# Attention scores on TensorE: eight 64x32 places taken in turn, in place of four

## The chip, the core and the metric

The kernel runs on one core of a Trainium2 chip. The metric is the device time of one execution in microseconds (us), as the median of several executions; lower is better. A profile of one execution shows what each engine did: PE is TensorE's matmul part and PEld its weight loads, DVE is VectorE, ACT ScalarE, POOL GpSimd, SP the engine that issues most DMAs. L525 is line 525 of the kernel.

## What is computed

A macaron block on x of shape (2, 1024, 128): half a step of a transformer, a linear recurrence with two projections, and half a step of the same transformer again. The transformer has six layers, run twice (12 layer passes). One layer, cut to what matters here:

```
def attn_layer(x, Wqkv, qs, ksc, Wo):         # 16 heads of 64, windows of 32
    q, k, v = split(x @ Wqkv)                  # after the token shift
    q, k = rotary(l2norm(q) * qs), rotary(l2norm(k) * ksc)
    # each window of 32 queries sees its own 32 keys and the 32 before them
    sim = einsum('bhwie,bhwje->bhwij', bq, bk2) * 8
    attn = softmax(where(mask, -max, sim))
    return einsum('bhwij,bhwje->bhwie', attn, bv2) @ Wo
x = attn_layer(shift_tokens(x), ...) + x
x = ffn_layer(shift_tokens(x), ...) + x        # layernorm, gated gelu
```

All of it is float32.

## The kernel before

The 2048 tokens are cut in 16 tiles of 128. A tile in one layer pass is a unit, 192 in all, and they go through a software pipeline that is written out in full: in step s every engine works on several units at different lags (constants `L_QKV` = 1, `L_S` = 2, `L_SM` = 3, `L_AV` = `L_WO` = 4, `L_F` = 5, `L_F2` = 6). A step, from the scores of one unit to those of the next, is one 192nd of the run apart from the ends. Engines run their own instruction streams in program order and meet at semaphores.

On TensorE a step (`step` in the `tensor` block, L544) issues in this order: the projections of chunks 1 and 0 (`project`, L479, proj bank c % 2), eight transposes of the rotated q (L493), `attend` (L529, the value products), the projections of chunks 2 and 3, eight transposes of k, the output projection (L593), eight transposes of the probabilities (L601), one of the normalised tile (L606), the second feed-forward product (L621), `values` (L488, two matmuls), a transpose of Z (L639), `hidden` (L501) and last `scores` (L512). Between them stand the waits for the other engines: the second projection waits for VectorE's hT (`v_h`), the second value matmul for VectorE's fourth rotation (L866, `v_ab[2]`).

On VectorE a step has four pairs of `rotate` (L860 and L866), the reductions of the squares (L953, L956), twelve small operations of the inverse root, hT (L990) once ScalarE's gelu (L739) is there, and then, when the scores are there (`p_S`), their row maximum (L997) and its subtraction (L1000). In the middle layers, some 24 steps from 1480 to 1900 us, the linear recurrence runs in between (L901 is its scan).

`scores`: a tile has four windows of 32 queries, w = 2*ty + g, with ty the half of the tile and g the window within it. A mask matmul in bf16 writes each of two PSUM banks, one for each ty. Then for each of 8 head pairs p there are 8 products, one for each window and each head hp of the pair: weights qT of 64 rows (the head's rows, hp*64 on) and 32 queries, moving kT of the same 64 rows and 64 keys; the result goes to 32 partitions of the score tile `sps` in bank ty.
The softmax works on rows, so it doesn't matter which head is in which quadrant. The probabilities are transposed to pT with the partition as the column, and `attend` takes 32 of those columns for a head, a window group g and a half t: weights v (64x64), moving pT (64x32), 64 products into two banks, t giving the row half and the bank.

Of the kernel before, what the change touches and what calls it, by code (L numbers as in the profile page):

```python
# [21 lines left out]
P = 128  # L22
DEPTH, HEADS, DH, WIN = 6, 16, 64, 32
# [34 lines left out]
def macaron(nc, x_in, w_in, w_out, b_out, w_qkv, q_scale, k_scale, w_o,  # L58
            w_1, w_2, b_2, c_cols, c_rope, c_mask, c_ident, out):
    with ExitStack() as ctx:  # L60
        def sb(name, shape, dt=F32):
            return ctx.enter_context(nc.sbuf_tensor(name, [P] + shape, dt))
# [10 lines left out]
        kT = sb("kT", [PAIRS, WIN + 2 * P])  # L73
        qT = sb("qT", [PAIRS, P])
# [52 lines left out]
        sps = ctx.enter_context(nc.psum_tensor("sps", [P, 2, 512], F32))  # L127
# [219 lines left out]
        for c in range(3):  # L347
            rows = min(FC, FH - c * FC)
# [117 lines left out]
        def _(pe):  # L466
            mm, tr = nc.tensor.matmul, nc.tensor.transpose
# [44 lines left out]
            def scores(k):  # L512
                first = k.off("first", L_S, lambda u: ((POS - 1 - u % POS) // (POS - 1)) * 512)
                par = k.parity(L_S)
                for ty in range(2):
                    m = mask[:, bass.ds(first, 512)] if ty == 0 else mask[:, 0:512]
                    mm(sps[:, ty, :], idb[:, :], m, start=True, stop=False, skip_group_check=True)
                for p in range(PAIRS):
                    for g in range(2):
                        for hp, ty in ((0, 0), (1, 1), (0, 1), (1, 0)):  # L520
                            w = 2 * ty + g
                            at = par * P + w * WIN  # L522
                            rows = slice(hp * DH, (hp + 1) * DH)
                            to = g * 64 + hp * WIN  # L524
                            last = mm(sps[to:to + WIN, ty, p * 64:p * 64 + 64], qT[rows, p, w * WIN:(w + 1) * WIN],  # L525
                                      kT[rows, p, at:at + 2 * WIN], start=False, stop=True, skip_group_check=True)
                last.then_inc(p_S, 1)

            def attend(k):  # L529
                par = k.parity(L_AV)  # L530
                for p in range(PAIRS):
                    for g in range(2):
                        for hp in range(2):
                            for t in range(2):
                                o4 = ops[:, t, p * 64:(p + 1) * 64].rearrange("p (g i) -> p g i", g=2)
                                at = (2 * p + hp) * DH
                                rows = slice(t * DH, (t + 1) * DH)
                                v = vb[rows, at:at + DH] if g == 0 else va[rows, par, at:at + DH]
                                to = (g * 2 + hp) * WIN
                                last = mm(o4[hp * DH:(hp + 1) * DH, g, :], v, pT[rows, p, to:to + WIN],  # L540
                                          start=True, stop=True, skip_group_check=True)
                last.then_inc(p_O, 1)

            def step(k):  # L544
# [30 lines left out]
                if k.on(L_AV):  # L575

                    attend(k)
# [69 lines left out]
                if k.on(L_S):  # L647

                    k.wait(v_sub, L_S + 1)
                    k.wait(v_rs, L_QKV, per=RS_STEPS)  # L650
                    k.wait(a_qT, L_S)
                    k.wait(a_kT, L_S)
                    if k.parity(L_S) == 0:
                        k.wait_even(a_car, L_S)
                    if k.reg is None and k.s == L_S:
                        pe.wait_ge(s_idb, 1)
                        pe.wait_ge(s_mask, 1)
                    scores(k)
# [558 lines left out]
```

## Time and profile before

| | |
|---|---|
| time, median of 3 runs | 3353.95 us (3350.72 to 3357.08) |
| the profiled execution: its run time | 3356.96 us |
| its span, first to last instruction | 3355.2 us |
| TensorE matmul busy | 3267.4 us (97%), 63272 instructions |
| weight loads busy | 2487.9 us (74%) |
| VectorE busy | 2756.8 us (82%) |
| ScalarE busy | 2542.9 us (76%) |
| GpSimd busy | 2225.8 us (66%) |
| scores, matmuls | 24576, 407.0 us busy |
| value products, matmuls | 24576, 751.3 us busy |

Busy time counts a stretch once however many matmuls are in flight in it, and the ends of matmuls are modelled: the mean of one scores matmul is 217 ns while one starts each 14 ns. So for small matmuls the start times are what to read. A matmul's row has the shape of its place in the array as rows*columns (64*32), then the moving operand's shape.

### The profile page before, as it was taken

To read this page: it belongs to the slowest core of one execution; us is meant where nothing else is said; L and a number is where in the kernel's file an instruction comes from. 1 tells how busy PE (TensorE), PEld (TensorE's weight loads), DVE (VectorE), ACT (ScalarE), POOL (GpSimd) and SP (SyncE) were. 2 spreads that over 40 slices of the span, in tenths; PEclk is the share of its full clock that TensorE was granted. 3 is DMA by queue.
4 is the path that set the end of the run, shared out by engine and by line. 5 is a ranking of instruction groups with operands and counts; after the bars stand their busy time and mean duration, and the time that the engine had idled before them with its cause. 6 is when DMAs were issued, how large, how long until landed. Compare 5 with 4: busy or idle time off the path is not lost. (4 is left out here: it accounts for less than half of the span.)

```text
span 3355.2 us, 150147 instructions
## 1 busy us (share of the span) xinstructions
PE 3267.4 (97%) x63272; PEld 2487.9 (74%) x63464; DVE 2756.8 (82%) x6951; ACT 2542.9 (76%) x4144; POOL 2225.8 (66%) x1453
## 2 busy tenths in 40 slices
PE   7999999999999999999999999999999999999998
PEld 4777777777777777777777777777777777777776
DVE  7888888888878888889999888788888888888885
ACT  3777777777777777777777777777777777777775
POOL 6666666666666666667887666666666666666663
PEclk9999999999999999999999999999999999999999
DMA  3111111111111111111111111111111111111111
GB/s 122 44 47 44 47 44 47 44 46 44 40 47 44 47 44 47 44 47 45 38 47 43 48 44 45 41 44 47 44 47 44 47 44 44 44 41 47 47 52 38
DMA packets 135089, 157.39 MB, mean 47 GB/s; under 512 B 75539, under 2 KB 108439, under 8 KB 134423
## 3 DMA queue, kind: packets, MB, share of 16 engines
q1 hardware_dynamic: 129815, 144.42, 15.6%
q8 instruction: 509, 8.34, 1.1%
q10 hardware_dynamic: 4608, 3.34, 0.3%
q14 instruction: 157, 1.29, 0.1%
HBM read 33.38 MB, written 1.05 MB: 10 GB/s over the span
## 5 line engine op out<-in xcount | busy, mean ns | idle before, releaser
L1073 POOL TENSOR_TENSOR rot<-rot,swp 128x1024 f32<-128x1024 f32 x384 | 906.6, 2361 | 133.8 <-DVE rot L866 133.8
L673 ACT ACTIVATE sq<-proj 128x512 f32<-128x512 f32 x768 | 437.7, 596 | 459.5 <-PE proj L482 448.9
L482 PE MATMUL proj<-wq,xsT 128*128 128x512 f32 x1536 | 768.7, 622 | 14.3 <-DVE rot L866 11.1
L1082 POOL TENSOR_TENSOR rot<-rot,rn 128x1024 f32<-128x1024 f32 x384 | 724.1, 1907 | 0.0
L1063 POOL TENSOR_TENSOR rt<-rt,half 128x1 f32<-128x1 f32 x192 | 105.3, 548 | 797.4 <-DVE rt L936 797.4
L860 DVE TENSOR_TENSOR swp<-proj,tab 128x512 f32<-128x512 f32 x768 | 521.1, 679 | 5.7 <-ACT sq L673 3.6
L866 DVE TENSOR_TENSOR rot<-proj,tab 128x512 f32<-128x512 f32 x768 | 517.6, 674 | 0.6 <-PE tps L493 0.6
L493 PEld LDWEIGHTS tps<-idf,rot 128*128 128x128 f32 x3072 | 359.7, 141 | 204.3 <-issue 202.5
L990 DVE SCALAR_TENSOR_TENSOR hT<-proj,cols,fg 114x128 f32<-114x128 f32 (+1 forms) x576 | 166.7, 345 | 416.9 <-ACT fg L739 412.8
L1067 POOL TENSOR_TENSOR prob<-prob,rr 128x1024 f32<-128x1024 f32 x192 | 365.4, 1903 | 175.3 <-DVE rr L948 175.3
L525 PEld LDWEIGHTS sps<-kT,qT 64*32 64x32 f32 x24576 | 365.4, 107 | 130.0 <-issue 129.6
L525 PE MATMUL sps<-kT,qT 64*32 64x64 f32 x24576 | 407.0, 217 | 38.6 <-issue 38.1
L482 PEld LDWEIGHTS proj<-wq,xsT 128*128 128x128 f32 x1536 | 259.5, 189 | 232.3 <-issue 142.3
L493 PE MATMUL tps<-idf,rot 128*128 128x128 f32 x3072 | 398.6, 273 | 2.3 <-POOL rot L1082 1.1
L540 PE MATMUL ops<-pT,vb 64*64 64x32 f32 x12288 | 377.6, 221 | 2.5 <-issue 2.3
L593 PE MATMUL ops<-wo,oT 128*128 128x128 f32 x3072 | 375.5, 276 | 2.4 <-ACT oT L695 2.4
L540 PE MATMUL ops<-pT,va 64*64 64x32 f32 x12288 | 373.7, 219 | 0.4 <-issue 0.4
L488 PE MATMUL proj<-wq,xsT 128*128 128x512 f32 x768 | 366.2, 598 | 3.4 <-DVE rot L866 3.3
L593 PEld LDWEIGHTS ops<-wo,oT 128*128 128x128 f32 x3072 | 358.9, 192 | 2.7 <-issue 2.6
L540 PEld LDWEIGHTS ops<-pT,vb 64*64 64x64 f32 x12288 | 328.6, 135 | 35.5 <-issue 35.2
L721 ACT COPY pT<-tps 128x1024 f32<-128x1024 f32 x192 | 194.4, 1012 | 186.4 <-PE tps L601 186.4
L540 PEld LDWEIGHTS ops<-pT,va 64*64 64x64 f32 x12288 | 329.8, 135 | 0.7 <-issue 0.6
(102 smaller groups left out, 5872.1 us busy)
## 6 DMA issues: line engine op xcount, KB each, us to landing
vb<-va SPq DMA_DIRECT2D x192, 384.0 KB, 3.5
vb<-va SPq DMA_DIRECT2D x192, 128.0 KB, 3.6
wq<-in_L_ffn_Wqkv SPq DMA_DIRECT2D x95, 192.0 KB, 3.4
xs<-Z SPq DMA_DIRECT2D x192, 32.0 KB
wo<-in_L_ffn_Wo SPq DMA_DIRECT2D x94, 64.0 KB, 2.8
xs<-Z SPq DMA_DIRECT2D x192, 28.0 KB
xs<-Z SPq DMA_DIRECT2D x192, 3.8 KB
xs<-Z SPq DMA_DIRECT2D x192, 0.2 KB
```

The costliest lines, as they stand in the source:

```text
L482: mm(proj[:, c % 2, :], xsT[:, k.parity(L_QKV), 0:P], wq2[:, bass.ds(w + c * 512, 512)], start=True, stop=True).then_inc(p_qkv[c], 1)
L488: mm(proj[:, c, :], xsT[:, k.parity(L_S), 0:P], wq2[:, bass.ds(w + (4 + c) * 512, 512)], start=True, stop=True).then_inc(p_v[c], 1)
L493: last = tr(tps[:, p, :], rot[:, g * INNER + p * P:g * INNER + (p + 1) * P], idf[:, :])
L525: last = mm(sps[to:to + WIN, ty, p * 64:p * 64 + 64], qT[rows, p, w * WIN:(w + 1) * WIN], kT[rows, p, at:at + 2 * WIN], start=False, stop= ...
L540: last = mm(o4[hp * DH:(hp + 1) * DH, g, :], v, pT[rows, p, to:to + WIN], start=True, stop=True, skip_group_check=True)
L593: last = mm(ops[:, 0, 0:P], oT[:, p, :], wo[:, bass.ds(w + p * P, P)], start=(p == 0), stop=(p == PAIRS - 1))
L673: fn(sq[:, c * 512:(c + 1) * 512], proj[:, c % 2, :], ACT.Square).then_inc(a_sq[c], 1)
L860: v.tensor_tensor(halves(swp[:, c * 512:(c + 1) * 512]), swapped, tab[:, bass.ds(po + (2 * g + 1) * POS * DH, DH)] .rearrange("p (a d) -> ...
L866: v.tensor_tensor(heads(rot[:, c * 512:(c + 1) * 512]), heads(src), tab[:, bass.ds(po + 2 * g * POS * DH, DH)].unsqueeze(1) .to_broadcast( ...
L1067: g_.tensor_tensor(pr, pr, rr[:, :].unsqueeze(2).to_broadcast([P, HEADS, 2 * WIN]), ALU.mult).then_inc(g_nrm, 1)
L1073: g_.tensor_tensor(r, r, swp[:, g * INNER:(g + 1) * INNER], ALU.add).then_inc(g_add[g], 1)
L1082: g_.tensor_tensor(r, r, rn[:, g * HEADS:(g + 1) * HEADS].unsqueeze(2) .to_broadcast([P, HEADS, DH]), ALU.mult).then_inc(g_nm[g], 1)
```

## The change

Two places. In `scores` the loops go over ty, then g, then hp, and the result of a product goes to quadrant 2*g + (hp xor ty). So the products of ty = 0 stay in their quadrants, those of ty = 1 swap theirs with the other head of the pair. A head pair's eight products now use eight different combinations of row half and quadrant, in turn. In `attend` the column of pT is taken from 2*g + (hp xor t) accordingly. Counts, shapes, waits and signals are as before.

```diff
                 for p in range(PAIRS):
-                    for g in range(2):
-                        for hp, ty in ((0, 0), (1, 1), (0, 1), (1, 0)):
-                            w = 2 * ty + g
-                            at = par * P + w * WIN
-                            rows = slice(hp * DH, (hp + 1) * DH)
-                            to = g * 64 + hp * WIN
-                            last = mm(sps[to:to + WIN, ty, p * 64:p * 64 + 64], qT[rows, p, w * WIN:(w + 1) * WIN],
-                                      kT[rows, p, at:at + 2 * WIN], start=False, stop=True, skip_group_check=True)
+                    for ty in range(2):
+                        for g in range(2):
+                            for hp in range(2):
+                                w = 2 * ty + g
+                                at, rows = par * P + w * WIN, slice(hp * DH, (hp + 1) * DH)
+                                to = (2 * g + (hp ^ ty)) * WIN
+                                last = mm(sps[to:to + WIN, ty, p * 64:(p + 1) * 64], qT[rows, p, w * WIN:(w + 1) * WIN],
+                                          kT[rows, p, at:at + 2 * WIN], start=False, stop=True, skip_group_check=True)
                 last.then_inc(p_S, 1)
...
-                                to = (g * 2 + hp) * WIN
+                                to = (2 * g + (hp ^ t)) * WIN
                                 last = mm(o4[hp * DH:(hp + 1) * DH, g, :], v, pT[rows, p, to:to + WIN],
                                           start=True, stop=True, skip_group_check=True)
```

## Rows read from the trace of the kernel before

**Rows 1.** The page: span, and busy us of each engine (share) x instructions.
```profile
span 3355.2 us, 150147 instructions
PE 3267.4 (97%) x63272; PEld 2487.9 (74%) x63464; DVE 2756.8 (82%) x6951; ACT 2542.9 (76%) x4144; POOL 2225.8 (66%) x1453
```

**Rows 2.** Timeline, 1256 to 1276: start us, us, engine line op [idle <-releaser].
```profile
1257.78 2.01 PE L525 MATMUL sps<-kT,qT 64*32 64x64 f32 x128
1258.75 0.87 DVE L990 SCALAR_TENSOR_TENSOR hT<-proj,cols,fg 114x128 f32<-114x128 f32 x3 [2.09 <-ACT fg L739]
...
1259.87 1.23 DVE L997 TENSOR_REDUCE mx<-sps 128x16 f32<-128x1024 f32 x1 [0.25 <-PE sps L525]
1260.26 0.19 PEld L482 LDWEIGHTS proj<-wq,xsT 128*128 128x128 f32 x1 [0.24 <-issue]
1260.69 0.19 PEld L482 LDWEIGHTS proj<-wq,xsT 128*128 128x128 f32 x1 [0.24 <-issue]
...
1270.68 0.68 DVE L866 TENSOR_TENSOR rot<-proj,tab 128x512 f32<-128x512 f32 x1
...
1271.41 0.39 PEld L488 LDWEIGHTS proj<-wq,xsT 128*128 128x128 f32 x2 [0.47 <-DVE rot L866]
...
1274.58 1.62 PE L525 MATMUL sps<-kT,qT 64*32 64x64 f32 x100
```

**Rows 3.** Waits over the whole run: waiting line <- releaser: us, times, longest.
```profile
DVE mx L997 <- PE sps L525: 109.1, 183, 4.3
...
PE sps L525 <- issue: 38.1, 57, 1.3
```

**Rows 4.** The scores' line: count, duration of one in ns, min/median/max.
```profile
L525 PE MATMUL sps<-kT,qT x24576: 212/216/242, 40.3 to 3321.0; 64*32 64x64 f32 x200
```

**Rows 5.** Timeline, 1500 to 1520: a step whose scores stop.
```profile
1512.98 1.34 PE L525 MATMUL sps<-kT,qT 64*32 64x64 f32 x79
...
1514.73 0.91 PE L525 MATMUL sps<-kT,qT 64*32 64x64 f32 x49 [0.41 <-issue]
...
1515.71 1.22 DVE L997 TENSOR_REDUCE mx<-sps 128x16 f32<-128x1024 f32 x1 [0.89 <-PE sps L525]
```

**Rows 6.** The page: DMA queue of TensorE's instructions, packets and MB.
```profile
q8 instruction: 509, 8.34, 1.1%
```

**Rows 7.** DMA queues, 1511.90 to 1513.26 alone.
```profile
q8 instruction: 1, 0.02, 6.1%
```

**Rows 8.** Timeline, a step of the middle layers, 1723.9 to 1741.
```profile
1726.02 0.87 DVE L990 SCALAR_TENSOR_TENSOR hT<-proj,cols,fg 114x128 f32<-114x128 f32 x3
1726.81 1.22 DVE L997 TENSOR_REDUCE mx<-sps 128x16 f32<-128x1024 f32 x1
1726.94 0.30 PEld L482 LDWEIGHTS proj<-wq,xsT 128*128 128x128 f32 x2 [0.65 <-DVE hT L990]
```

**Rows 9.** Windows, L525 alone: stretch, its us, PE busy (matmuls in flight), clock, DMA.
```profile
1760.27:1760.31 0.04, 0.04 (x4) 1.00 0.09 2
1760.32:1760.33 0.01, 0.01 (x6) 1.00 0.04 1
1760.35:1760.36 0.01, 0.01 (x8) 1.00 0.00 0
1760.37:1760.39 0.01, 0.01 (x10) 1.00 0.00 0
...
1760.43:1760.44 0.01, 0.01 (x14) 1.00 0.00 0
```

**Rows 10.** Windows, L540 alone, a phase that starts at 1782.32: PE, then PEld.
```profile
1782.34:1782.37 0.03, 0.03 (x4) 0.03 (x4) 1.00 0.00 0
1782.39:1782.42 0.03, 0.03 (x8) 0.03 (x8) 1.00 0.00 0
```

**Rows 11.** Timeline, first and last group of the value products' weight loads, one step.
```profile
1500.91 0.21 PEld L540 LDWEIGHTS ops<-pT,vb 64*64 64x64 f32 x8 [0.17 <-issue]
...
1502.65 0.21 PEld L540 LDWEIGHTS ops<-pT,va 64*64 64x64 f32 x8
```

## Prediction

 A step takes 3355.2/192 = 17.5 us on average, this one 16.8 (scores at 1257.78, the next at 1274.58). The last work of a step on TensorE is the scores: 128 matmuls from 1257.78 to 1259.79. VectorE finishes hT at 1259.62, waits 0.25 us and starts its row maximum at 1259.87. From there VectorE runs nearly without a pause to its fourth rotation (end 1271.36), which releases the second value product (its weights wait until 1271.41), and values, copy, table load, gelu and hT lead back to the maximum. So TensorE and VectorE are bound together: VectorE's ring would close 0.25 us sooner if the scores were ready, and no more than that.
>
> The totals say the same: VectorE waits 109.1 us for the scores, 183 times, 0.57 us per step. Much of it isn't the scores' own length: 57 times TensorE stands still on this line with nothing that releases it, 38.1 us in all [rows 3]. In one such step the scores stop after 79 matmuls, for 0.41 us, and VectorE then waits 0.89 us instead of 0.25 [rows 5]. The instruction queue brings 16 KB blocks (8.34 MB in 509 packets) [rows 6], and one arrives in the 1.4 us before these scores [rows 7]. I read the stops as waits for instructions. In the middle layers VectorE has a scan besides, hT ends after the scores, and TensorE waits for hT [rows 8].
>
> **The change, part by part.** The matmul count, their shapes (64x32 weights, 64 moving columns), the waits and the signals stay. What differs: (a) the products of the second half of the windows (ty = 1) swap their column quadrant, so the sequence on TensorE goes over eight (row half, quadrant) places and not twice over each of two, then twice over the other two; (b) the order within a head pair is ty, group, head; four products in a row now write the same PSUM bank, where before the bank changed with every other product; (c) the value products read pT at columns swapped for t = 1.
>
> (c) costs nothing: the moving operand is the same 32 columns of the same 64 rows, and the mask and the copy to oT don't depend on which head sits in which quadrant. It has no cover: value products and projections follow each other on TensorE without a gap, so a dearer one would be paid in full. (b) I cost by the start of one scores phase [rows 9]: product 4 (bank 0, upper rows) is followed within 0.03 us by product 5 (bank 0, lower rows). Product 3 comes over 0.03 us after product 2, both in bank 1, which a collision would explain, but so does the place that product 3 shares with product 1. So 0, with the collision below as its upper bound.
>
> (a) is the change. What does a product cost now? In an undisturbed step 128 matmuls (64 products of two passes) span 2.01 us with the last one's 0.216 [rows 2, 4]: 1.79/127 = 14.1 ns each, 28.2 ns per product, 56.4 ns per product of one row half. A full-array matmul of 512 columns takes 0.43 us (two weight loads of the projection start at 1260.26 and 1260.69 [rows 2]), 0.84 ns per column. At that rate the two passes of 64 columns take 107 ns. The scores thus run twice as fast as one row half could go serially, and there are two readings:
> - Reading A: a place is busy 107 ns, and a row half runs its two quadrants side by side; 2 x 107 = 214 ns of each 4 x 56.4 = 226 ns are used, so places are full and eight would halve the time.
> - Reading B: a row half takes in a product every 56 ns, whatever quadrant it goes to; eight places change nothing.
>
> The trace can separate them where a phase starts on an empty array. Products 1 and 3 go to the same place, product 5 to one not yet used, 7 again to that one. In flight are 4 matmuls until 1760.31, 6 from 1760.32, 8 from 1760.35, 10 from 1760.37 and 14 from 1760.43 [rows 9]. Two matmuls are a product: product 3 starts at about 1760.31, 5 between 1760.36 and 1760.37, 7 between 1760.41 and 1760.43. Product 5 finds its place empty and still comes 0.055 us behind product 3, just as product 7 comes 0.055 us behind product 5 in the same place. The value products say it again: the first four matmuls are in by 1782.34, the next four, for a quadrant pair not yet used in this phase, only after 1782.37 [rows 10]; over the whole phase eight loads (four products) go in each 0.116 us (16 such groups, 1500.91 to 1502.65 [rows 11]), 29.0 ns per product. Against B speaks only that both cases use exactly two column places per row half, so A's factor two fits both. I take B: a free place that is left unused is seen directly, a matching factor isn't. Term: 0 per step and in sum; the bounds on both sides are the rivals' prices.
>
> The Trainium skill has a rule on either side. Its page "TensorE: Matmul & The Clock Gate" (Part 3: Packing small matmuls) says that weight loads overlap matmuls in flight only when the row group differs; by that the two row halves set the pace and the sum stays 0. "TensorEngine Tiling (Array Packing)" (Tiling Modes) lists 64x32 as eight independent tiles that load and multiply in parallel; by that the sum would be the gain of the first rival. The row on product 5 agrees with the former.
>
> Sum: 3355.2 us span of the profiled execution, run time 3357.0, the median of three 3354.0; so 3357.0 + 0 there, and against the median 3354.
>
> **The rivals.** First, reading A: eight places, scores in about half (0.9 us less TensorE time per step). It isn't worth 192 x 0.9 = 173 us. In undisturbed steps VectorE can start the maximum at most when hT ends. In a middle step it starts even 0.08 us before that (1726.81, hT's end being 1726.89) [rows 8], so the gain is 0.25 + 0.08 = 0.33 us. 57 of the 192 steps have a stop [rows 3], which ends when the instructions arrive, so only the matmuls behind it gain: 49 x 7 ns = 0.34 us in the step of [rows 5]; half of that, 0.17 us, I take as the mean, since a stop can fall on any later matmul. The 24 middle steps gain nothing. Of the other 168, 118 are undisturbed, x 0.33 = 39 us, and 50 stopped, x 0.17 = 8 us: 47 us, 3307 us. The ceiling is all of VectorE's wait, 109.1 us, 3245; a partial speed-up to 20 ns per product still saves 0.5 us per step and so gives the same 39 us in the undisturbed steps. For it: the full-array rate. Against: products 5 and 7.
>
> Second, slower: row halves that share a quadrant. Before, quadrants 0 and 2 belong to the lower row half, 1 and 3 to the upper one, and the other half never loads weights into them. The value products use each quadrant pair from both halves, and there four loads and four matmuls are in by 1782.34 and nothing follows for 0.03 us [rows 10]. If the sharing is what keeps loads and matmuls apart, each pair of products costs a load of 32 columns (32 x 0.84 = 27 ns) more: 32 x 27 ns = 0.86 us per step. It decides as soon as the scores end after hT, thus in all undisturbed steps: 118 x 0.86 = 101 us; in the 50 stopped ones the part behind the stop, a quarter, 11 us: 112 us, 3466. The mild form, the value products' 29.0 ns per product in place of 28.2, is 0.05 us per step, in 168 steps 9 us, 3363. Against it: the wider weights (64 columns) explain the value products without any sharing.
>
> Third, slower too: a bank written by both row halves. The Trainium skill's "PSUM — Partial Sum Buffer" quotes that different row tiles can't access the same bank at once. Of that page the rival needs nothing: if neighbours in one bank stood 56 ns apart in place of 28, and not only the 32 pairs that share one now but 48 of 64 did, 16 x 28 ns = 0.45 us per step would be added, on 118 steps 53 us, 3407. Products 4 and 5 speak against it [rows 9]; no row here shows four in a row.
>
> **How the numbers follow.** No change (B): 0.63, of which 0.01 falls outside 0.2%. Reading A: 0.26. Shared quadrants: 0.07, of which 0.02 is the mild form. Shared bank: 0.04. The likeliest gives 3354, its own range 3347 to 3362 (the three runs spread over 3350.7 to 3357.1, and the stops can shift a little). For 8 in 10 the range has to reach into A: 3296 takes in most of it, and 3368 takes in the mild slower form. A difference under 0.2% (7 us) can't be told from none. Faster 0.27, same 0.62, slower 0.11.
>
> **What would show it.** Right: the scores of an undisturbed step still span about 2.0 us, product 5 still starts 0.055 us behind product 3, the maximum still waits 0.25 us, and the total wait for the scores stays near 109 us. Reading A: 128 matmuls in 1.1 to 1.5 us, the maximum starting right at the end of hT, its wait down to some 60 us and all of that in stopped steps, with TensorE waiting for hT or a rotation instead. Shared quadrants: scores of 2.1 to 2.9 us, with weight loads and matmuls in separate bursts. Shared bank: gaps of 56 ns between neighbours. What would make the forecast wrong above all is that the evenness of products 5 and 7 comes from the order in which the queue lets loads pass, and not from the row halves.

## The result, and the profile after

| | before | after |
|---|---|---|
| median of 4 runs each, same chip | 3355.14 us (3350.72 to 3357.08) | 3319.09 us (3317.88 to 3320.53) |
| profiled execution: run time, span | 3356.96, 3355.2 us | 3317.88, 3316.0 us |
| ratio, 95% interval | | 0.9895, 0.9877 to 0.9912 |

The kernel became 36 us faster, where no change was forecast as likeliest. The time lies inside the stated range (3296 to 3368), in the part that had been kept for the first rival. The same kernel was run twice more, on two other chips, each time beside the kernel before: 3304.88 us against 3350.86 (0.9867, 0.9852 to 0.9881) and 3303.78 against 3348.05 (0.9864, 0.9848 to 0.9880), so 44 to 46 us there.

First the page of after, span and busy time, which answers to [rows 1]:

```profile
span 3316.0 us, 150147 instructions
PE 3177.3 (96%) x63272; PEld 2384.7 (72%) x63464; DVE 2748.5 (83%) x6951; ACT 2545.5 (77%) x4144; POOL 2226.4 (67%) x1453
```

Same instructions, and TensorE's matmuls are busy 90 us less (3267.4 before), of which 39 us reach the span. An undisturbed step in the timeline of after, which answers to [rows 2] (start us, us, engine line op, idle and releaser):

```profile
1289.81 1.48 PE L525 MATMUL sps<-kT,qT 64*32 64x64 f32 x128
1290.78 0.87 DVE L990 SCALAR_TENSOR_TENSOR hT<-proj,cols,fg 114x128 f32<-114x128 f32 x3 [2.43 <-ACT fg L739]
...
1291.57 1.21 DVE L997 TENSOR_REDUCE mx<-sps 128x16 f32<-128x1024 f32 x1
1291.91 0.19 PEld L482 LDWEIGHTS proj<-wq,xsT 128*128 128x128 f32 x1 [0.24 <-DVE hT L990]
...
1306.17 1.07 PE L525 MATMUL sps<-kT,qT 64*32 64x64 f32 x85
...
1307.64 0.68 PE L525 MATMUL sps<-kT,qT 64*32 64x64 f32 x43 [0.41 <-issue]
...
1308.36 1.22 DVE L997 TENSOR_REDUCE mx<-sps 128x16 f32<-128x1024 f32 x1 [0.35 <-PE sps L525]
```

128 matmuls take 1.48 us with the last one's 0.216, in place of 2.01: 1.26/127 = 10 ns each, 20 ns per product, where it was 28. The row maximum no longer waits: it starts 0.08 us before hT's end (1290.78 + 0.87 = 1291.65), as in the middle steps of before [rows 8]. The next projection's weights now wait for hT, so the two engines have changed places. The next scores start at 1306.17, 16.36 us on. They stop after 85 matmuls, and the maximum waits 0.35 us for them.

The waits over the whole run, after (waiting line <- releaser: us, times, longest), which answer to [rows 3]:

```profile
DVE hT L990 <- ACT fg L739: 413.6, 179, 4.2
...
DVE mx L997 <- PE sps L525: 71.4, 70, 3.9
PE sps L525 <- issue: 71.4, 68, 1.8
...
PEld proj L482 <- DVE hT L990: 34.3, 112, 1.4
```

This is the account of the change. VectorE's wait for the scores falls from 109.1 us in 183 steps to 71.4 us in 70, by 37.7 us, and the span falls by 39.2. Counted step by step in the two traces (start of one scores phase to the start of the next), the 103 steps outside the middle layers whose scores stop in neither kernel give 31.5 us, and their median falls from 16.80 to 16.42 us; the 64 that stop in either give 2.7 us, and the 24 of the middle layers 4.0 us. Before, 183 - 57 = 126 of these waits had no stop, and at 0.25 us each they held 32 us; all of them are gone. What is left, 71.4 us, falls in steps whose scores stop. The stops themselves grew, from 38.1 us in 57 steps to 71.4 in 68. A second stopped step of after, with its DMA queue between 1271 and 1275, shows how (this answers to [rows 5] and [rows 7]):

```profile
1271.88 1.42 PE L525 MATMUL sps<-kT,qT 64*32 64x64 f32 x121
...
1274.70 0.31 PE L525 MATMUL sps<-kT,qT 64*32 64x64 f32 x7 [1.41 <-issue]
...
1275.07 1.22 DVE L997 TENSOR_REDUCE mx<-sps 128x16 f32<-128x1024 f32 x1 [1.36 <-PE sps L525]
```
```profile
q8 instruction: 1, 0.02, 2.2%
```

TensorE has done 121 of 128 matmuls and stands 1.41 us before the last seven. A block of instructions comes in between 1271.73 and 1273.13 us, 1.57 us before TensorE goes on. That this is no accident shows in all stops of the list: in each of the 57 of before and the 68 of after, TensorE goes on 1.2 to 1.6 us after the end of a packet of the instruction queue, of which there is one in about 6.5 us (509 in the span). The mean stop went from 0.67 us (38.1/57) to 1.05 (71.4/68): a faster engine gets to the end of what it has been sent sooner, and the block comes no sooner for that. Stops aren't confined to the scores: gaps of over 0.2 us between two starts of the value products' matmuls hold 5.1 us in 10 cases before and 11.0 us in 16 after.

### The profile page after: what moved, and what is told of

Same layout as the page of the kernel before. It is cut to its first block and busy times, and to the rows that moved or that the text cites. A ratio compares the mean times of both kernels' runs of the same rounds, so it can differ in the third digit from the quotient of the medians.

```text
span 3316.0 us, 150147 instructions
## 1 busy us (share of the span) xinstructions
PE 3177.3 (96%) x63272; PEld 2384.7 (72%) x63464; DVE 2748.5 (83%) x6951; ACT 2545.5 (77%) x4144; POOL 2226.4 (67%) x1453
## 3 DMA queue, kind: packets, MB, share of 16 engines
q8 instruction: 509, 8.34, 1.1%
HBM read 33.38 MB, written 1.05 MB: 10 GB/s over the span
## 5 line engine op out<-in xcount | busy, mean ns | idle before, releaser
L540 PE MATMUL ops<-pT,vb 64*64 64x32 f32 x12288 | 378.6, 220 | 5.1 <-issue 4.9
L540 PE MATMUL ops<-pT,va 64*64 64x32 f32 x12288 | 376.7, 219 | 2.5 <-issue 2.3
L525 PEld LDWEIGHTS sps<-kT,qT 64*32 64x32 f32 x24576 | 260.0, 105 | 163.2 <-issue 163.0
L525 PE MATMUL sps<-kT,qT 64*32 64x64 f32 x24576 | 302.9, 225 | 71.6 <-issue 71.4
L540 PEld LDWEIGHTS ops<-pT,vb 64*64 64x64 f32 x12288 | 329.2, 134 | 38.2 <-issue 38.0
L540 PEld LDWEIGHTS ops<-pT,va 64*64 64x64 f32 x12288 | 331.4, 135 | 3.2 <-issue 2.7
```

Source lines behind the costliest of these rows:

```text
L525: last = mm(sps[to:to + WIN, ty, p * 64:(p + 1) * 64], qT[rows, p, w * WIN:(w + 1) * WIN], kT[rows, p, at:at + 2 * WIN], start=False, stop ...
```

## Experiments

Each kernel was timed against the kernel before on the same chip. "Phase" is the time from the first to the last matmul start of the scores in an undisturbed step: 1.80 us before, 1.27 after.

### Is it the number of places, or the order?

The change did two things at once: eight places in place of four, and another order. The first two kernels do one each, with the column of pT in `attend` taken accordingly.

e1: the new order, but the old four places.

```diff
-                                to = (2 * g + (hp ^ ty)) * WIN
+                                to = (2 * g + hp) * WIN
```

> The changed kernel's loop order (half, window, head) with the quadrants of the kernel before, so four places in turn and each is used again after four products. Places theory (a place is busy some 107 ns per product and only their number counts): 28 ns per product, 128 matmuls in about 2.0 us, 3354 us. Reuse theory (the loss before came from using a place again two products later): nearly as fast as the change, some 1.5 us per phase, 3320 us. Partner theory (fast when neighbours read the same columns of q and k and write one bank): as fast as the change, 3319 us.

3335.36 us (3329.69 to 3339.81), ratio 0.9960 (0.9947 to 0.9974); phase 1.78 us.

e2: the old order, with its alternating banks, and eight places.

```diff
-                            to = g * 64 + hp * WIN
+                            to = (2 * g + (hp ^ ty)) * WIN
```

> The eight places of the change, but in the order of the kernel before: neighbours are of different windows and different banks, and two row halves follow each other in one quadrant. Places theory: as fast as the change, 128 matmuls in about 1.5 us, 3319 us. Reuse theory: the same, since every place is used again only after eight products. Partner theory: slow, 2.0 us, 3354 us. Shared-quadrant cost (my slower rival): between them or above 3354.

3304.82 us (3301.93 to 3308.37), ratio 0.9872 (0.9858 to 0.9887); phase 1.27 us. Timelines of e1, then e2, an undisturbed step each:

```profile
1253.52 1.99 PE L525 MATMUL sps<-kT,qT 64*32 64x64 f32 x128
1254.49 0.87 DVE L990 SCALAR_TENSOR_TENSOR hT<-proj,cols,fg 114x128 f32<-114x128 f32 x3 [2.10 <-ACT fg L739]
1255.58 1.22 DVE L997 TENSOR_REDUCE mx<-sps 128x16 f32<-128x1024 f32 x1 [0.22 <-PE sps L525]
```
```profile
1266.31 1.51 PE L525 MATMUL sps<-kT,qT 64*32 64x64 f32 x128
1267.28 0.87 DVE L990 SCALAR_TENSOR_TENSOR hT<-proj,cols,fg 114x128 f32<-114x128 f32 x3 [2.30 <-ACT fg L739]
1268.06 1.22 DVE L997 TENSOR_REDUCE mx<-sps 128x16 f32<-128x1024 f32 x1
```

The places do most of it: e2 gains 43 us on this chip, all that the change gains, e1 13 us. Of e1's 13 us its maximum, which waits 0.22 us in place of 0.25, explains some 4, and 49 stops in place of 57 (33.1 us against 38.1) some 5; the other 4 are not explained. In e2 both row halves write the same quadrant one right after the other, and it costs nothing.

What remained was that the eight-place kernels also give neighbouring products other windows, thus other columns and partners. e3 keeps four places with neighbours of one window; e4 has eight with the windows mixed.

```diff
-                    for ty in range(2):
-                        for g in range(2):
+                    for g in range(2):
+                        for ty in range(2):
...
-                                to = (2 * g + (hp ^ ty)) * WIN
+                                to = (2 * g + hp) * WIN
```

> Four places as before, used again after two products as before, but neighbours are now of one window and one bank. Places theory and reuse theory: as slow as before, 2.0 us per phase, 3354 us. Partner theory: as fast as the change, 3319 us.

```diff
-                        for g in range(2):
-                            for hp in range(2):
+                        for hp, g in ((0, 0), (1, 1), (0, 1), (1, 0)):
```

> Eight places in turn and four products in a row in one bank, as in the change, but neighbours are of different windows, so that they read different columns of q and k. Places and reuse theory: as the change, 1.5 us per phase, 3319 us. Partner theory with the columns as its cause: 3354 us; with the bank as its cause: 3319 us.

e3 took 3349.89 us, ratio 1.0007 (0.9998 to 1.0016), with the phase of before; e4 3306.78 us, 0.9877 (0.9861 to 0.9894), with the phase of after. Three orders with eight places have a phase of 1.27 us, three with four places one of 1.78 to 1.80. Windows, partners and bank don't matter, and the order takes at most 0.02 us off a phase (e1); the places do.

### What the start of a phase tells

The forecast went by the first matmuls of a phase. Windows on the scores' line alone, from the start of one phase, in after (stretch, its us, PE busy with matmuls in flight, clock, DMA), then in e1:

```profile
1289.81:1289.83 0.02, 0.02 (x4) 1.00 0.00 0
1289.81:1289.87 0.06, 0.06 (x8) 1.00 0.00 0
1289.81:1289.91 0.10, 0.10 (x12) 1.00 0.00 0
1289.81:1289.95 0.14, 0.14 (x17) 1.00 0.00 0
```
```profile
1253.52:1253.54 0.02, 0.02 (x3) 1.00 0.00 0
1253.52:1253.58 0.06, 0.06 (x4) 1.00 0.00 0
1253.52:1253.62 0.10, 0.10 (x7) 1.00 0.00 0
1253.52:1253.66 0.14, 0.14 (x9) 1.00 0.00 0
```

The first four products (eight matmuls) go to the same four places in both kernels, in the same order, and each place is empty. After 0.06 us eight matmuls are in with after, and four with e1. The prediction counted two starts in a row as the two passes of one product. Counted so, the third product of e1 would be held in an empty place, and the same product in after would not, although the kernels differ only in what comes behind it. So that count can't be right in both, unless what comes behind a product holds it up, and a late start is no sign that the product's place is busy, nor that its row half is. No row of a trace names the product that a start belongs to.

The starts themselves, one by one in the traces, fall into a plain pattern. In e1 four matmuls start within 0.020 us, the next four from 0.080 us, then four in each 0.056 us to the end of the phase. In before it is also four in each 0.056 us. In after eight start within 0.047 us, and then eight from each of 0.080, 0.136 and 0.192 us. The first 0.25 us of a phase, in after and in e1:

```profile
1289.81:1290.06 0.25, 0.25 (x32) 1.00 0.00 0
```
```profile
1253.52:1253.77 0.25, 0.25 (x17) 1.00 0.00 0
```

### How long a place is held

Two kernels leave the second 32 keys of each product out of the scores (32 moving columns in place of 64), so they compute something else; e9 has eight places, e10 the four and the order of before:

```diff
-... sps[to:to + WIN, ty, p * 64:(p + 1) * 64] ... kT[rows, p, at:at + 2 * WIN] ...
+... sps[to:to + WIN, ty, p * 64:p * 64 + WIN] ... kT[rows, p, at:at + WIN] ...
```

> The changed kernel with 32 moving columns per score product in place of 64: the second 32 keys of each window are left out of the scores. The matmul count stays. Places theory: a place is busy 53 ns, so eight places allow 7 ns per product. If the changed kernel's phase of 1.27 us between its first and last start is still set by its places, it falls to under 1.0 us; if it is set by the number of instructions, it stays at 1.2 to 1.3 us.

> The kernel before (four places, each used twice in a row) with 32 moving columns per score product in place of 64: the second 32 keys of each window are left out of the scores. Places theory: its 1.80 us from the first to the last start fall to the floor that instructions set, 1.0 to 1.3 us, since a place is busy half as long. If the row half or the queue sets the pace whatever the columns, it stays at 1.6 to 1.8 us.

e9: 3308.86 us (one run), phase 1.10 us. e10: 3296.24 us (one run), phase 1.21 us. Timelines, e9 then e10:

```profile
1313.94 1.29 PE L525 MATMUL sps<-kT,qT 64*32 64x32 f32 x128
```
```profile
1275.64 1.40 PE L525 MATMUL sps<-kT,qT 64*32 64x32 f32 x128
```

With four places, half the columns take a third off the phase, 1.80 to 1.21 us: four places are held by the columns that run through them. With eight they take off 0.17 us (1.27 to 1.10). So eight places are near another limit, some 17 to 20 ns per product, which has little to do with columns. In e9, too, the first 32 matmuls start within 0.16 us; then nothing starts for 0.08 us, and soon two start in each 0.017 us, up to the end. Which limit it is these runs don't tell. Both kernels end near 3300 us for all that they leave out, since they have 66 and 64 stops and their undisturbed steps, 16.42 us at the median, are as long as those of after.

### What the stops are, and what they cost

If a stop is a wait for the next block of instructions, it goes by where in the stream a block ends, not by what TensorE does. The queue's 8.34 MB in 509 packets [rows 6] are 16 KB each, and a step has 676 instructions on TensorE (counted in the program: matmuls, weight loads, semaphores), so a block holds about 192 x 676/509 = 255 of them; I take 256. The position of a block's end so moves from step to step, in three steps by 3 x 676 = 8 x 256 - 20, thus 10 matmuls on. The stops do just that: in after they come at matmul 85, 95, 105, 115 and 125 of the scores in steps 11, 14, 17, 20 and 23 (the first is step 0). None in before or after comes ahead of matmul 79. e6 puts about 22 products of 8 columns in front of the xn transpose, so that a step has 768 instructions and the boundary stays some 60 instructions into the scores. e7 has the same number in nearly all steps (36 filler products fewer in the whole run), but the boundary some 205 in.

```diff
+            def filler(k):
+                for n in range(FILL[k.s - L_S] if k.s - L_S < T else 0):
+                    hp = n % 2
+                    to = (2 * (n // 2 % 2) + hp) * WIN
+                    rows = slice(hp * DH, (hp + 1) * DH)
+                    mm(sps[to:to + WIN, 1, 0:8], idf[rows, 0:WIN], idf[rows, 0:8], start=True, stop=True,
+                       skip_group_check=True)
```

> The changed kernel with some 22 small products per step (64x32 weights, 8 moving columns, result overwritten by the next transpose) put ahead of the transpose of the normalised tile, so that a step has 768 instructions on TensorE and every third block boundary of 256 falls some 60 instructions into the scores. Fetch theory (the stops are waits for a block of instructions, asked for too late when a boundary falls in the second half of the scores): the stops of the scores go, 71.4 us to under 10 us, at a cost of 0.4 to 0.7 us of TensorE time per step of which VectorE's ring hides 0.2: 3270 to 3340 us. If the stops have another cause: 71 us of stops remain and the time rises to 3330 to 3400 us.

> The same filler products, but five more or fewer per step near the start, so that the boundary falls some 205 instructions into the scores of every step. Fetch theory: nearly every step has a stop of 1 to 2 us, 190 or so in place of 68, 200 to 300 us of them, and 3500 us or more. Another cause: as the kernel with the boundary at 60.

e6: 3336.46 us (3334.83 to 3338.93), ratio 0.9961 (0.9946 to 0.9975). e7: 3446.23 us (two runs, 3443.74 and 3448.72), 1.0288 (1.0267 to 1.0308). Waits of e6, then of e7:

```profile
DVE hT L1000 <- ACT fg L749: 513.4, 179, 4.2
...
DVE mx L1007 <- PE sps L526: 10.3, 4, 3.9
...
PE sps L526 <- issue: 2.8, 2, 1.5
```
```profile
DVE hT L1000 <- ACT fg L749: 513.6, 178, 4.2
...
PE sps L526 <- issue: 104.1, 118, 1.8
DVE mx L1007 <- PE sps L526: 98.9, 117, 4.2
```

The same work but for those 36 products, shifted: the stops go from 2 to 118, and the time by 110 us. In e7 all but one of the 128 gaps of over 0.2 us between two starts lie at matmul 101, 102 or 103 of 128 (starts in the trace; the list of waits leaves the ten shortest out); in after they are spread from matmul 79 to 127. With the packets above that settles what they are. I had expected one in each step of e7 and over 3500 us. In 64 of 192 steps there was no such gap, so whether a block is late has a second condition. The trace shows it, though not its cause: in all 128 steps with a gap a packet of the instruction queue starts between 1.11 us before and 0.56 us after the scores' start, and in the other 64 none does; there the last packet, if there was one, starts at least 2.2 us ahead of the scores. Why it is asked for at two different times stays open. The price of a stop is 0.95 us: 110/116.

The fillers themselves cost: hT waits 513 us for gelu in place of 414, 0.5 us per step, because they lie on the way to gelu. So e6 without stops isn't faster than after with them.

### Where the gain would be without them

e5 leaves out the scores of head pairs 4 to 7, in after:

```diff
-                for p in range(PAIRS):
+                for p in range(PAIRS // 2):
```

> The changed kernel with the score products of the second four head pairs left out, 64 matmuls per step in place of 128. If VectorE's ring sets the undisturbed step, its length stays at 16.6 us although TensorE has 0.6 us less work; the time falls only by what is left of the stops, 50 to 75 us. If TensorE still sets it, 0.6 us per step, 115 us or more go.

3225.2 us (one run). Its timeline:

```profile
1255.00 0.86 PE L525 MATMUL sps<-kT,qT 64*32 64x64 f32 x64
1255.97 0.87 DVE L990 SCALAR_TENSOR_TENSOR hT<-proj,cols,fg 114x128 f32<-114x128 f32 x3 [2.35 <-ACT fg L739]
1256.75 1.22 DVE L997 TENSOR_REDUCE mx<-sps 128x16 f32<-128x1024 f32 x1
...
1271.36 0.86 PE L525 MATMUL sps<-kT,qT 64*32 64x64 f32 x64
```

TensorE has 0.6 us less to do per step, and the step takes 16.36 us here, like the shortest of after; outside the middle layers its median step is 16.42 us, and that of after's undisturbed steps is 16.42 too. The maximum starts 0.09 us before hT's end again. So a faster scores phase gives next to nothing more: VectorE's ring sets about 16.4 us. e5 has no stops in its scores. VectorE's wait for them is 5.5 us in all, against 64.5 in the two later runs of after, so 59 of the 80 us by which it is below them are that (on another chip, and in one run); the rest isn't split up.

Could the stops be had off without a longer ring? Four kernels cut the scores in two parts around the feed-forward product `hidden`, so that part of them runs where more slack was thought to be. e8 puts the ty = 1 products ahead of hidden and ty = 0 behind; e11 puts ty = 1 between its two halves. A part has four places.

```diff
+                    scores(k, 1)
                 if k.on(L_F):
...
                         hidden(k, a)
+                if k.on(L_S):
+                    scores(k, 0)
```

> The changed kernel with the products of the second half of the tile ahead of the hidden products and those of the first half behind them. Each part has four places in turn. Fetch theory: 28 matmuls of 128 columns (1.6 us) now lie inside the dense stretch, so stops fall from 71 us to under 40 us. Places theory: each part runs at 28 ns per product, 1.8 us in all, so TensorE gives back 0.5 us per step and VectorE's wait in steps without a stop is 0.25 us again. Together 3300 to 3345 us.

> The scores in two parts as in the kernel that splits them, but the gate's hidden products (three of six) go ahead of the first part, so that ScalarE's gelu is not kept waiting; the other three stand between the parts. If VectorE's ring (fourth rotation, second value product, copy, table load, gelu, hT, maximum) sets the undisturbed step and the stops are instruction fetches, the step falls from 16.83 to about 16.55 us and the stops stay under 40 us: 3255 to 3290 us. If 0.8 us between the parts is too little for the fetch, stops of up to 1 us come back in some 70 steps: 3300 us.

e8: 3314.36 us (3312.56 to 3316.22), ratio 0.9895 (0.9879 to 0.9912). e11: 3344.83 us (3342.08 to 3347.80), 0.9983 (0.9973 to 0.9992). Timelines, e8 then e11:

```profile
1256.65 1.10 PE L526 MATMUL sps<-kT,qT 64*32 64x64 f32 x64
...
1258.62 0.88 ACT L744 ACTIVATE fg<-proj,cols 114x128 f32<-114x128 f32 x3 [0.31 <-PE proj L501]
...
1259.39 1.10 PE L526 MATMUL sps<-kT,qT 64*32 64x64 f32 x64
```
```profile
1267.94 0.89 ACT L746 ACTIVATE fg<-proj,cols 114x128 f32<-114x128 f32 x3
...
1268.99 0.87 DVE L997 SCALAR_TENSOR_TENSOR hT<-proj,cols,fg 114x128 f32<-114x128 f32 x3 [2.48 <-PE proj L501]
1269.10 0.94 PEld L526 LDWEIGHTS sps<-kT,qT 64*32 64x32 f32 x64 [0.32 <-issue]
1269.10 1.10 PE L526 MATMUL sps<-kT,qT 64*32 64x64 f32 x64
1270.27 1.23 DVE L1004 TENSOR_REDUCE mx<-sps 128x16 f32<-128x1024 f32 x1 [0.40 <-PE sps L526]
```

e8 has next to no stops (1.1 us in 4), and gelu waits 0.31 us for hidden in each step instead. e11 has few (3.8 us in 15) and gelu is in time, but with four places per part and a second change-over (0.32 us ahead of the loads) the scores end after hT again, and the maximum waits 0.40 us. hT itself now waits for TensorE's second half of hidden (421.5 us in 179 steps) and no more for gelu. I had given e11 3255 to 3290.

The last two keep eight places and cut by head pairs: pairs 0 to 3 between the halves of hidden and pairs 4 to 7 at the end (e12), or pairs 0 to 3 ahead of both halves (e13).

```diff
-                for p in range(PAIRS):
+                for p in range(half * PAIRS // 2, (half + 1) * PAIRS // 2):
...
-                    for a in (1, 0):
-                        k.wait(a_v[a], L_S)
-                        hidden(k, a)
+                    k.wait(a_v[1], L_S)
+                    hidden(k, 1)
...
-                    scores(k)
+                    scores(k, 0)
+                if k.on(L_F):
+                    k.wait(a_v[0], L_S)
+                    hidden(k, 0)
+                if k.on(L_S):
+                    scores(k, 1)
```

> Eight places as in the changed kernel; both mask loads and the scores of head pairs 0 to 3 go out behind hidden(1), then hidden(0), then head pairs 4 to 7. If the gain that is missing is held back by instruction waits alone and either half of the split keeps the eight places' rate: the steps take 16.4 to 16.55 us (VectorE's ring, at which the kernel with half the scores runs), VectorE waits for scores under 20 us in all, and the time is 3230 to 3290 us. If TensorE is the bound whichever way the phase is cut, as in the kernel split at the same point by windows: steps of 16.9 us, a VectorE wait of 60 to 90 us, 3320 to 3350 us. If the wait for hidden(0) at ScalarE's gelu counts: ScalarE shows it on the second gelu, and the step is 16.8 as in the other split.

> As the one before, but head pairs 0 to 3 go out ahead of both halves of hidden. If gelu's release by hidden(1) sets ScalarE's stream, the 0.7 us of scores in front of it shows as a wait of 0.3 us before the first gelu of each step, the step is 16.8 us and the time 3310 to 3320, as in the kernel with the windows split around hidden. If that wait is absorbed, 16.5 us and 3250 to 3290. If stops were the whole of what was lost in the changed kernel, this one shows hardly any and is below 3260.

The kernel after ran a second time between these groups and a third time beside the last two:

> The changed kernel itself, to stand beside the others on one chip. Every theory: about 0.9895 of the kernel before.

> The changed kernel once more, beside the two above: 3300 to 3322 us, with 60 to 70 stops of 1 us.

They gave the 3304.88 and 3303.78 us of the first section.

e12: 3305.77 us (3303.71 to 3308.51), beside 3303.78 for after. e13: 3434.45 us (3433.04 to 3437.05), ratio 1.0259 (1.0244 to 1.0274). Waits of e12, then of e13:

```profile
DVE mx L1002 <- PE sps L525: 58.9, 70, 3.9
PE sps L525 <- issue: 42.7, 69, 1.5
```
```profile
DVE hT L995 <- ACT fg L744: 603.0, 179, 4.4
...
ACT fg L744 <- PE proj L501: 208.5, 191, 2.1
PE sps L517 <- issue: 120.0, 184, 0.9
```

e12 misses its 3230 to 3290. Cutting the scores in two leaves 69 stops in them, though shorter ones: 42.7 us, against 63.7 in 64 for after on the same chip. Its undisturbed steps outside the middle layers take 16.56 us at the median, against 16.42 for after, so TensorE isn't the bound at 16.9, but the cut costs 0.14 us, about what the shorter stops give back. Gelu doesn't wait, but hT now waits for TensorE's second half of hidden (423.9 us in 179 steps) and no more for gelu (409.4 us in 178 for after). e13 misses by far more. There the scores' own wait, for VectorE's inverse root, comes ahead of hidden: TensorE stands 0.65 us (120.0/184) in front of the mask, then does 1.3 us of mask and scores, and gelu waits 1.09 us (208.5/191) in each step. Most of that goes into the step, which takes 17.5 us. This is why hidden comes first.

No kernel that computes the whole was faster than after beyond its interval; e2, e4 and e12 are level with it.

## Why the prediction was wrong

**What bounds the kernel** held. VectorE's ring and TensorE were bound together, with 0.25 us between them, and when the scores got shorter the maximum stopped waiting, at 0.08 us before hT's end, as the middle step had shown.

**Term (a), 0 per step, failed.** It measured 36 to 46 us over the run. The step that failed is the choice of reading B, that a row half takes in a product every 56 ns whatever quadrant it goes to, by [rows 9, 10]: "product 5 finds its place empty and still comes 0.055 us behind product 3". The start times are right, but that two starts in a row are one product is shown by no row, and e1 beside after speaks against it: there the same four products on the same four empty places make four starts or eight within 0.06 us. A start at the head of a phase doesn't tell what a place or a row half can take. What the runs showed in its place is that the number of places sets the pace: one matmul per place starts in each 56 ns, with four places through the whole phase and with eight for its first 32 matmuls, and the phase goes from 1.80 to 1.27 us. The prediction's own last sentence named this danger, an order that comes from the queue and not from the row halves. The test I set aside was the better one: the full-array rate gives 107 ns per place, of which the four places used 214 of each 226 ns. That factor fitted both readings, but B had only it and the starts, and no row showed a row half on two alternating places faster than one. Near-full occupancy should have weighed more than the order of five starts.

The rule on row groups, from the Trainium skill's "TensorE: Matmul & The Clock Gate" (Part 3: Packing small matmuls), was cited as agreeing with B. In e1 against after the row groups alternate alike and only the quadrants differ, and the phase goes from 1.78 to 1.27 us: as a pace for these products the rule doesn't hold here. "TensorEngine Tiling (Array Packing)" (Tiling Modes), with eight independent 64x32 tiles, is the one that the measurement bears out, though not in full: eight in place of four gave twice the rate for the first 32 matmuls only, and 1.4 times over the phase.

**Terms (b) and (c), 0 each, held.** Alternating or equal banks make no difference (e2 against e4: 0.9872 and 0.9877), and the value products' phase is as it was, 1.85 us from first to last start at the median of both traces.

**The first rival** had the mechanism and nearly the sum: 47 us and 3307 forecast, 36 us on the first chip and 44 to 46 on two others. By its parts: it gave undisturbed steps 0.33 us, and 0.25 + 0.08 is what the timelines show; the median step fell by 0.38. Its "partial speed-up to 20 ns per product still saves 0.5 us" is the one that came, 0.53 us. Its signs came as well: 128 matmuls in 1.48 us, the wait down to 60 to 70 us and all in stopped steps, TensorE waiting for hT. It gave 39 us to undisturbed steps, 8 to stopped ones and nothing to the middle layers; measured were 31.5, 2.7 and 4.0. What it missed is that a stopped step gains hardly anything, 0.04 us in place of 0.17: the stops grow as TensorE gets to them sooner (38.1 us in 57, then 71.4 in 68). In the two later runs the stops are shorter (63.5 and 63.7 us in 64), and the same count against the trace of before, from another chip, gives the stopped steps 13 and 11 us. The near hit was partly luck: scores in half the time were assumed and 0.53 of 0.9 us came, which did no harm because VectorE's ring is what holds an undisturbed step from there on. One outcome can't grade a chance, but with the occupancy at 214 of 226 ns, 0.26 was low.

**The slower rivals** fell. Shared quadrants cost nothing (e2), nor does a bank that four neighbours share (e4, level with e2, whose neighbours alternate).

**The stops** were read rightly as waits for instructions, which e6 and e7 show, and were underrated. They now hold 64 to 71 us, about all that is left of the wait for the scores. The Trainium skill's "Runtime: NRT & Kernel Launch" says in its section on instruction fetch mechanics that the crossing from one block to the next is mostly hidden. Here, in a stretch of 256 short instructions in 1.5 us, it isn't: 0.95 us for each stop, of which e7 has 118.

**Still open:** what sets the 17 to 20 ns per product with eight places, from the 33rd matmul of a phase on; why the block is asked for early enough in 64 of e7's steps and not in the others; and whether the 64 us can be had by shifting the block ends without filler on the way to gelu.

## What to carry to other kernels

Price the gain by the wait behind it: here 0.53 us per step of TensorE was worth 0.38 us, and 0.04 where an instruction block was late. In a dense stretch of short instructions look for "issue" waits, see where they fall, and what a few instructions more or less do to them.

## What was not expected of the hardware

- On the same four empty places, with the same first four products, eight matmuls start within 0.06 us when four more places follow, and four when the same four follow again (windows of after and e1).
- With eight places exactly 32 matmuls start at the full pace in every phase, within 0.24 us; the others come at some 0.7 of it (after, e2, e4).
- After a stop TensorE goes on 1.2 to 1.6 us after the end of an instruction packet, in all 243 stops of before, after and e7.
- With four places a phase of 64 products goes from 1.80 to 1.21 us when the columns are halved, with eight only from 1.27 to 1.10.
- The position of a block's end, with nearly the same work, moves the time by 110 us, 3.3% (e6 against e7).
- The same kernel stood at 0.9895 of the kernel before on one chip and at 0.9867 and 0.9864 on two others.
